# V weights loaded uncast by SyncE and cast on VectorE, in a linear-attention block on eight cores

## The reference

```python
q = phi(xn @ W_Q.T); k = phi(xn @ W_K.T); v = xn @ W_V.T      # 8 heads of 64; phi(u) = elu(u) + 1
S = gamma * S + k (outer) v;  z = gamma * z + k               # scan over the tokens, gamma = sigmoid(decay_log)
y = (S.T q) / (z . q + 1e-6) * sigmoid(xn @ W_g.T + b_g)
attn = y @ W_O.T
w = top-2 of softmax(xn @ gate_w.T)
ffn = xn @ W_lin.T + b_lin + sum over the two experts of w * (xn @ left_e) @ right_e     # rank 4
out = x + attn + ffn
```

## Time and profile before

| what | value |
|---|---|
| median of three runs | 260.21 us |
| the profiled execution's own time | 260.27 us |
| span of its slowest core (core 3) | 259.2 us |
| spans of the eight cores | 256.0 to 259.2 us |
| TensorE busy | 236.6 us (91%) |
| VectorE, ScalarE, GpSimd busy | 162.0, 75.5, 61.7 us |
| granted TensorE clock, all cores | 1.000 |

### The profile page before, as it was taken

How to read it: one execution, slowest core, us unless ns; L and a number is a source line. 1 busy time by engine, 2 the same in 40 slices (tenths; PEclk the granted TensorE clock), 3 DMA queues, 4 the chain that set the end, 5 groups by cost and what they waited for, 6 DMA issues and landing times.

```text
span 259.2 us, 5279 instructions; the slowest of 8 cores (256.0 to 259.2 us)
## 1 busy us (share of the span) xinstructions
PE 236.6 (91%) x1688; PEld 116.9 (45%) x1688; DVE 162.0 (63%) x425; ACT 75.5 (29%) x128; POOL 61.7 (24%) x99
## 2 busy tenths in 40 slices
PE   0238999999989999999999999999999999999995
PEld 0124354454545555454444455444545454445442
DVE  3743667658848678666555657556656776677522
ACT  2653766476163432314132021112110201000000
POOL 0790300012144421405050403021304030333000
PEclk9999999999999999999999999999999999999999
DMA  5999999999998046342435122223231315243423
GB/s 147 237 153 263 250 167 188 252 174 177 232 199 266 3 116 192 61 164 61 164 41 170 37 82 83 101 82 104 82 124 63 121 63 181 82 153 104 154 106 137
DMA packets 20366, 35.86 MB, mean 138 GB/s; under 512 B 12210, under 2 KB 12530, under 8 KB 20084
## 3 DMA queue, kind: packets, MB, share of 16 engines
q1 hardware_dynamic: 17444, 24.89, 32.0%
q0 software_dynamic: 2896, 10.64, 21.7%
HBM read 32.00 MB, written 8.39 MB: 156 GB/s over the span
## 4 chain that ended last, share of the span: by engine, by line
PE 85%; DMA 6%; DVE 3%; issue 2%; ACT 2%; DVEq 0%; ACTq 0%; POOLq 0%
PE PJ L367 27%; PE L L389 17%; PE L L433 9%; PE PJ L360 8%; DMA wv_sb<-wv 5%; PE PJ L389 4%; PE L L367 3%; PE PJ L433 2%; PE SY L381 2%; DMA x_sb<-x 2%; PE SY L405 2%; PE T L419 1%; PE SY L409 1%; PE T L338 1%; PE T L427 1%
## 5 line engine op out<-in xcount | busy, mean ns | idle before, releaser
L389 PE MATMUL L<-wlin_sb,xnfm 128*128 128x512 bf16 x208 | 49.2, 379 | 0.0
L325 POOL TENSOR_SCALAR S_blk<-S_sb,small_s 128x260 bf16<-128x260 f32 x30 | 28.6, 969 | 82.7 <-DVE S_sb L827 82.5
L389 PEld LDWEIGHTS L<-wlin_sb,xnfm 128*128 128x128 bf16 x208 | 20.0, 98 | 24.4 <-issue 1.0
L656 DVE TENSOR_SCALAR e_sb<-e_sb 128x512 bf16<-128x512 bf16 x32 | 9.7, 302 | 30.7 <-ACT e_sb L898 30.7
L898 ACT ACTIVATE e_sb<-PJ 128x512 bf16<-128x512 f32 x28 | 16.5, 593 | 40.5 <-PE PJ L367 39.4
L367 PE MATMUL PJ<-xnfm,wk_sb 128*128 128x512 bf16 x112 | 26.6, 380 | 1.2 <-ACT th_g L905 1.2
L874 ACT ACTIVATE xn_tm<-x_sb,nmr,rstd 128x1024 bf16<-128x1024 f32 x16 | 19.9, 1242 | 25.4 <-POOL nmr L281 23.9
L433 PE MATMUL L<-wo_sb,ygfm 128*128 128x512 bf16 x104 | 26.7, 379 | 0.0
L367 PE MATMUL PJ<-xnfm,wg_sb 128*128 128x512 bf16 x112 | 26.6, 379 | 0.0
L367 PE MATMUL PJ<-xnfm,wq_sb 128*128 128x512 bf16 x112 | 26.6, 380 | 0.0
L360 PE MATMUL PJ<-wv_sb,xnfm 128*128 128x512 bf16 x96 | 23.7, 389 | 2.5 <-DMA wv_sb<-wv 2.5
(11 more groups left out here) (122 smaller groups left out, 336.7 us busy)
## 6 DMA issues: line engine op xcount, KB each, us to landing
ro_sb<-x SPq DMA_DIRECT2D x16, 512.0 KB, 3.4
out<-ro_sb SPq DMA_DIRECT2D x15, 512.0 KB, 2.7
x_sb<-x SPq DMA_DIRECT2D x10, 512.0 KB, 8.4
x_sb<-x POOLq DMA_DIRECT2D x6, 512.0 KB, 21.6
wlin_sb<-wlin POOLq DMA_DIRECT2D x1, 2048.0 KB, 38.5
wv_sb<-wv POOLq DMA_DIRECT2D x4, 256.0 KB, 12.7
wq_sb<-wq POOLq DMA_DIRECT2D x2, 512.0 KB, 18.5
wk_sb<-wk POOLq DMA_DIRECT2D x2, 512.0 KB, 25.4
```

Of the source, the lines that this page charges most:

```text
L325: GP.tensor_scalar(S_blk[:, :].rearrange("p (q w) -> p q w", q=4)[:, :, 65 * e : 65 * e + 65], S_sb[:, :].rearrange("p (q w) -> p q w", q= ...
L389: TE.matmul(lb(c, n)[:, :], xnk(k, c), wlin_sb[:, D * k + 512 * n : D * k + 512 * n + 512], start=False, stop=False)
L656: VE.tensor_scalar(e_sb[:, 512 * i : 512 * i + 512], e_sb[:, 512 * i : 512 * i + 512], 1.0, None, ALU.min).then_inc(dv_m, 1)
```

## The change

The V weights no longer come through GpSimd's queue. SyncE loads them as fp32 in two halves of 1 MB each, one between x 2 and x 3 and one behind x 3, into the space of `wlin_sb`, which holds nothing yet. VectorE casts them in four quarters to `wv_sb` (`cast_wv`). The constants stand behind them on SyncE's queue. GpSimd's queue starts with the first half of Q once the first half of V has landed; W_lin and W_O wait for the four casts and are issued ahead of the two small copies. TensorE's V phase is ordered anew: chunks 0, 1 and 2 take the first half of the weights as they come, then all take the second. The work on constants is spread: the `nlg` steps stand around `xn(4)` and `xn(5)`, `dk8`, `gc4` and `dpq` behind the exponentials of Q, the eight exponent operations of the mask behind Q's last `phi` and ahead of `stats(6)`, and the mask's exponential behind `xn(7)` and ahead of K's first exponential. The first scores wait for the mask in the loop.

```diff
--- before.py
+++ after.py
@@ -88,6 +88,7 @@
     small = A("small_s", [128, 19], F32)
     cmat = th_g[:, 0:384]
     mtmp = th_g[:, 2048:3072]
+    wv32 = wlin_sb[:, :].bitcast(F32)
     bl32 = th_g[:, 3072:4096]
     nlg = A("nlg", [128, 12], F32)
     gc4 = A("gc4", [128, 4], F32)
@@ -136,13 +137,14 @@
     d_r = [sem(f"d_r{c}") for c in range(NCH)]
     d_id, d_sm, d_cm, d_bl = sem("d_id"), sem("d_sm"), sem("d_cm"), sem("d_bl")
     d_lg = sem("d_lg")
-    d_wv, d_wq, d_wk, d_wg = ([sem(f"d_wv{i}") for i in range(4)], [sem("d_wqa"), sem("d_wqb")],
+    d_wv, d_wq, d_wk, d_wg = ([sem("d_wva"), sem("d_wvb")], [sem("d_wqa"), sem("d_wqb")],
                               [sem("d_wka"), sem("d_wkb")], [sem("d_wga"), sem("d_wgb")])
     d_wl, d_wo, d_rt = sem("d_wl"), sem("d_wo"), sem("d_rt")
     pe_xtr, pe_v, pe_q, pe_k, pe_g = (sem("pe_xtr"), sem("pe_v"), sem("pe_q"), sem("pe_k"),
                                       sem("pe_g"))
     pe_tg, pe_tht, pe_ktr, pe_sc = sem("pe_tg"), sem("pe_tht"), sem("pe_ktr"), sem("pe_sc")
     pe_av, pe_st, pe_ytr, pe_o = sem("pe_av"), sem("pe_st"), sem("pe_ytr"), sem("pe_o")
+    dv_cast = sem("dv_cast")
     dv_ini, dv_st, dv_bn, dv_xev = sem("dv_ini"), sem("dv_st"), sem("dv_bn"), sem("dv_xev")
     dv_dec, dv_mk, dv_tgc = sem("dv_dec"), sem("dv_mk"), sem("dv_tgc")
     dv_one, dv_nm, ac_ln, dv_rt = sem("dv_one"), sem("dv_nm"), sem("ac_ln"), sem("dv_rt")
@@ -217,11 +219,18 @@
         def load_res(c):
             SY.dma_start(ro(c), x_d[128 * c : 128 * c + 128, :]).then_inc(d_r[c], 16)
 
+        def load_wv(hf):
+            o = 4 * FH * hf
+            SY.dma_start(wv32[:, o : o + 4 * FH],
+                         wv_d[:, o : o + 4 * FH]).then_inc(d_wv[hf], 16)
+
         load_x(0)
         load_x(1)
         SY.dma_start(ident[:, :], ident_d[:, :]).then_inc(d_id, 16)
         load_x(2)
+        load_wv(0)
         load_x(3)
+        load_wv(1)
         SY.dma_start(small[:, :], small_d[:, :]).then_inc(d_sm, 16)
         SY.dma_start(cmat, cmat_d[:, :]).then_inc(d_cm, 16)
         SY.dma_start(bl32[32:33, 0:512], blin_d[:, 0:512]).then_inc(d_bl, 16)
@@ -283,10 +292,7 @@
 
     def pool_program():
         GP.memset(mhalf[:, :], -0.5).then_inc(po_ini, 1)
-        GP.wait_ge(d_x[0], 16)
-        for i in range(4):
-            o = 2 * FH * i
-            GP.dma_start(wv_sb[:, o : o + 2 * FH], wv_d[:, o : o + 2 * FH]).then_inc(d_wv[i], 16)
+        GP.wait_ge(d_wv[0], 16)
         wload_half(wq_sb, wq_d, 0, d_wq)
         xload(4)
         xload(5)
@@ -306,14 +312,15 @@
                          blin_d[:, 512 * n : 512 * n + 512]).then_inc(d_rt, 16)
         xload(8)
         xload(9)
+        GP.wait_ge(dv_cast, 4)
+        wload(wlin_sb, wlin_d, d_wl)
+        wload(wo_sb, wo_d, d_wo)
         GP.wait_ge(po_ini, 1)
         GP.wait_ge(ac_dec, 3)
         GP.tensor_copy(gC[:, :].rearrange("p (q w) -> p q w", q=4),
                        gc4[:, :].unsqueeze(2).to_broadcast([128, 4, 65]))
         GP.tensor_copy(dpk[:, :].rearrange("p (h w) -> p h w", h=8),
                        dk8[:, :].unsqueeze(2).to_broadcast([128, 8, 64])).then_inc(po_dk, 1)
-        wload(wlin_sb, wlin_d, d_wl)
-        wload(wo_sb, wo_d, d_wo)
         rs(8)
         rs(9)
         for c in range(NCH):
@@ -484,18 +491,22 @@
         xtr(0)
         xtr(1)
         TE.wait_ge(dv_xev, 1)
+        for i in range(2):
+            TE.wait_ge(dv_cast, i + 1)
+            vproj(0, ring4[0], 2 * i, 2 * i + 2)
         xtr(2)
         TE.wait_ge(dv_xev, 2)
-        TE.wait_ge(d_wv[0], 16)
-        for c in range(4):
-            if c == 3:
-                xtr(3)
-            TE.wait_ge(dv_xev, c + 1)
-            vproj(c, ring4[c], 0, 2)
-        for i in range(1, 4):
-            TE.wait_ge(d_wv[i], 16)
-            for c in range(4):
-                vproj(c, ring4[c], 2 * i, 2 * i + 2)
+        vproj(1, ring4[1], 0, 4)
+        TE.wait_ge(dv_xev, 3)
+        vproj(2, ring4[2], 0, 4)
+        for i in range(2, 4):
+            TE.wait_ge(dv_cast, i + 1)
+            vproj(0, ring4[0], 2 * i, 2 * i + 2)
+        xtr(3)
+        vproj(1, ring4[1], 4, 8)
+        vproj(2, ring4[2], 4, 8)
+        TE.wait_ge(dv_xev, 4)
+        vproj(3, ring4[3])
         TE.wait_ge(d_wq[0], 16)
         for m in range(4):
             TE.wait_ge(ac_v, m + 1)
@@ -650,6 +661,11 @@
         VE.tensor_copy(xdst(c), TT[c % 2][:, :].rearrange("p (k w) -> p k w", k=KCH)
                        ).then_inc(dv_xev, 1)
 
+    def cast_wv(i):
+        o = 2 * FH * i
+        VE.wait_ge(d_wv[i // 2], 16)
+        VE.tensor_copy(wv_sb[:, o : o + 2 * FH], wv32[:, o : o + 2 * FH]).then_inc(dv_cast, 1)
+
     def phi(n, bank, dst, s):
         i = n % 2
         VE.wait_ge(ac_e, n + 1)
@@ -732,17 +748,29 @@
         stats(1)
         stats(2)
         xev_v(0)
+        cast_wv(0)
+        cast_wv(1)
+        xev_v(1)
         stats(3)
-        xev_v(1)
         xev_v(2)
+        cast_wv(2)
+        cast_wv(3)
         xev_v(3)
+        stats(4)
         VE.wait_ge(d_sm, 16)
         VE.tensor_scalar(gb_h[:, :], small[:, 0:4], 0.5, None, ALU.mult).then_inc(dv_ini, 1)
+        stats(5)
         VE.wait_ge(ac_dec, 1)
         VE.tensor_scalar(nlg[:, :], nlg[:, :], 1e15, None, ALU.min).then_inc(dv_dec, 1)
+        xev_v(4)
+        for m in range(2):
+            phi(m, ring4[m], fm(qfm, 0)[:, 512 * m : 512 * m + 512], dv_q)
         VE.wait_ge(ac_dec, 2)
         VE.tensor_scalar(dk8a[:, :], nlg[:, 0:8], small[:, 16:17], None,
                          ALU.mult).then_inc(dv_dec, 1)
+        xev_v(5)
+        for m in range(2, 4):
+            phi(m, ring4[m], fm(qfm, 0)[:, 512 * m : 512 * m + 512], dv_q)
         VE.wait_ge(d_cm, 16)
         for h in range(H):
             o = (h % 2) * 512 + (h // 2) * 128
@@ -750,17 +778,9 @@
                                           nlg[:, h : h + 1], cmat[:, 128:256],
                                           ALU.mult, ALU.add)
         ins.then_inc(dv_mk, 1)
-        stats(4)
-        stats(5)
-        xev_v(4)
-        for m in range(2):
-            phi(m, ring4[m], fm(qfm, 0)[:, 512 * m : 512 * m + 512], dv_q)
-        xev_v(5)
-        for m in range(2, 4):
-            phi(m, ring4[m], fm(qfm, 0)[:, 512 * m : 512 * m + 512], dv_q)
         stats(6)
         stats(7)
-        VE.wait_ge(ac_mk, 1)
+        VE.wait_ge(ac_dec, 3)
         qt(0)
         for m in range(4):
             phi(4 + m, ring4[(m + 2) % 4], fm(kfm, 0)[:, 512 * m : 512 * m + 512], dv_k)
@@ -789,6 +809,8 @@
             if c > 0:
                 VE.wait_ge(pe_st, c)
             VE.tensor_tensor(ktm_sb[:, :], ktile, dpk[:, :], ALU.mult).then_inc(dv_ktm, 1)
+            if c == 0:
+                VE.wait_ge(ac_mk, 1)
             VE.wait_ge(pe_sc, c + 1)
             VE.tensor_tensor(A_sb[:, 0:512], SYb[0][:, :], masks[:, 0:512], ALU.mult)
             VE.tensor_tensor(A_sb[:, 512:1024], SYb[1][:, :], masks[:, 512:1024],
@@ -923,10 +945,17 @@
         SE.activation(dum[:, :], one_c[:, :], AF.Exp)
         for c in range(4):
             xn(c)
+        for c in range(4):
+            vev(c, ring4[c])
+        xn(4)
         SE.wait_ge(dv_ini, 4)
         SE.activation(nlg[:, :], small[:, 4:16], AF.Exp, scale=-1.0).then_inc(ac_dec, 1)
+        xn(5)
         SE.wait_ge(dv_dec, 1)
         SE.activation(nlg[:, :], nlg[:, :], AF.Ln, bias=one_c[:, :]).then_inc(ac_dec, 1)
+        for m in range(4):
+            SE.wait_ge(pe_q, m + 1)
+            eexp(m, ring4[m])
         SE.wait_ge(dv_dec, 2)
         SE.activation(dk8[:, :], dk8a[:, :], AF.Exp)
         SE.activation(gc4[:, :], nlg[:, 8:12], AF.Exp, scale=-128.0)
@@ -935,19 +964,12 @@
             ins = SE.activation(dpq[:, 128 * p : 128 * p + 128], cmat[:, 256:384], AF.Exp,
                                 scale=nlg[:, 8 + p : 9 + p])
         ins.then_inc(ac_dec, 1)
-        SE.wait_ge(dv_mk, 1)
-        SE.activation(masks[:, :], mtmp, AF.Exp).then_inc(ac_mk, 1)
-        for c in range(4):
-            vev(c, ring4[c])
-        xn(4)
-        xn(5)
-        for m in range(4):
-            SE.wait_ge(pe_q, m + 1)
-            eexp(m, ring4[m])
         vev(4, ring4[0])
         vev(5, ring4[1])
         xn(6)
         xn(7)
+        SE.wait_ge(dv_mk, 1)
+        SE.activation(masks[:, :], mtmp, AF.Exp).then_inc(ac_mk, 1)
         for m in range(4):
             SE.wait_ge(pe_k, m + 1)
             eexp(4 + m, ring4[(m + 2) % 4])
```

## The result

The changed kernel takes 263.59 us, the median of four runs (263.19 to 263.66), against 260.02 before in the same runs: 1.0144 times as long, 95% interval 1.0115 to 1.0174. It is slower by 3.6 us, and just outside the predicted range of 257.8 to 263.2.

What follows compares the result with a forecast made beforehand. Bound: two transfers, then a chain almost wholly on TensorE. Q starting 3.5 us earlier and constants adding 3.6 gave +0.1: span 259.3, plus 1.07 makes 260.4 us, no change; range 257.8 to 263.2.

Steps and rivals of the forecast that it cites:

- V's gain: V's weights by the new loading: V starts at 14.7 instead of 18.61 and Q at 25.2, 3.5 us earlier.
- T: The moment TensorE starts Q: 28.67 on core 3 before, predicted 25.2, with 230.5 us behind it before.
- the sum: Earlier start of Q, -3.5 us, plus constants put in behind it, +3.6: +0.1, span 259.3, time 260.4.
- the third rival: V's second half lands late because GpSimd's queue starts within 1 us and takes turns: T 27.9, time 263.1; chance 0.15.
- The price of the constants: Constants on the chain from Q's last phi to G: 3.6 us against 0.15 to spare, delaying G by that.
- the first rival: Constants behind T fall into slack of VectorE and ScalarE: 256.8, or 258.9 where 1.5 us hides; chance 0.2.
- x 4: Input chunk 4 on GpSimd's queue: claimed to come 2.9 us earlier with that queue, with some 2 us or more to spare.
- G - T: Time from TensorE's first Q matmul to its first G matmul: 19.6 us before, predicted 23.1 to 23.2.
- The clock: TensorE's clock falls after idling ahead of G, slowing G's first matmuls: +1.7 us, time 262.1; a rival, chance 0.15.
- its cases: 261.5 is the top of the forecast's own range, T at 26.3; 262.1 is the rival where TensorE's clock falls.
- its own range: The forecast's range for T from 24.2 to 26.3: time 259.2 to 261.5.

Runs made afterwards that it cites:

- e10: Changed kernel with the mask's exponents behind qt(0), its exponential behind K's, and V's weights back on GpSimd's queue in DMA-cast quarters; 259.34 us, 0.9984 times before.
- e9: Changed kernel with the mask's exponents behind qt(0), its exponential behind K's, and Q's weights started once x 0 landed, not V's first half; 265.29 us.
- e3: Kernel before with only the changed kernel's order of constants, including the earlier issue of W_lin and W_O; V's weights as before; 264.76 us, 1.0200 times before.
- e6: Kernel before with the constants' new order, but the mask's exponents behind qt(0) and its exponential behind K's; 260.36 us, 1.0026 times before.
- e8: Changed kernel with the mask's exponents behind qt(0), its exponential behind K's, and x 4 loaded ahead of Q's first half; 258.06 us, 0.9911 times before.
- e2: Changed kernel with 7 useless matmuls behind xtr(6) and 9 behind xtr(7), keeping TensorE busy ahead of G; 261.29 us.
- e4: Changed kernel with only the mask's exponential moved behind K's four exponentials, its exponents still ahead of stats(6); 261.25 us.

## Why the prediction was wrong

**V's gain was right.** Predicted: V at 14.7, Q at 25.2, halves landing at 13.9 and 19.2. Measured on core 7: 15.24, 25.55, and casts beginning at 14.40 and 19.41 as the halves landed. Two casts took 1.29 us, so 0.7 each was right. In part the size was luck. The 3.5 us were counted from core 3, the latest of the kernel before both in V and in Q. In the mean of the eight cores V starts 1.6 us sooner (16.4 to 14.8) and Q 2.6 (27.3 to 24.7), and by e10 about half of the gain in T is the order of the V phase, which the sum didn't price. GpSimd's packets came behind SyncE's, and the third rival didn't happen. e9 shows that the mechanism was real; its price of 263.1 can't be held against e9's 265.3, as q0's packets begin at 11.23 on core 3 of e9 and the rival had them at 14.9.

**The price of the constants was right.** 3.6 us predicted; 23.20 - 19.59 = 3.6 in e3, and 3.36 against the 19.84 of e6. There was nothing to hide it, and the first rival, to which 0.2 was given, is out.

**x 4 was wrong.** The step "everything on q0 comes 2.9 us earlier ... Chunks 4 to 7, K and G shift alike and had some 2 us or more to spare". On core 7 `stats(4)` starts at 25.40, having waited 2.33 us. The same core in the kernel before:

```profile
25.31 0.69 DVE L639 BATCH_NORM_STATS2 bn<-x_sb 128x6 f32<-128x512 f32 x1 [0.55 <-DMA x_sb<-x]
```

So x 4 came no sooner at all: it lands at 23.8 to 26.3 over the cores before and 24.0 to 26.1 after, 24.7 in the mean of both. The first half of Q's weights came 0.5 us sooner on core 7 (23.9 to 23.4). There was nothing to spare either: four cores already waited for x 4 in the kernel before, 0.3 to 1.1 us, and core 3 had 0.5. What did come sooner was its user: VectorE was free for `stats(4)` at 23.07 instead of 24.76 on core 7, and at 22.87 instead of 26.82 on core 3. In both kernels as many bytes are read ahead of x 4, and the DMA engines of core 7 are busy for 94 to 110% of every 2 us from 8 to 24; that fits, though no run tests it alone. The late x 4 made G - T 23.71 instead of 23.2 on core 7 and up to 25.1 elsewhere. e8 takes it away.

**The clock was the failed step.** The sum added 3.6 us to the 230.5 behind T and left the clock at nothing; it was put as a rival with 0.15, beside the forecast. It was a consequence of the forecast: the prediction had itself worked out 4.5 us with 1 us of work on TensorE, and both kernels with that stretch (the changed one, e3) lost the clock on six to eight cores in every execution. The price was +1.7. The difference to e2's time is 2.3 us. Core 7 leaves 213.2 us behind G, against 211.3 on the same core both before and in e2; six other cores and those of e3 leave 212.0 to 212.5 against core 3's 210.9, 1.1 to 1.6 more. The prediction's 234.1 us behind T held only where the clock did (234.6 on core 5; 235.7 to 237.1 on the others). Against it the text set only that no such gap stood in the trace of before, which speaks for neither side.

The sum with what was measured, on core 7: 25.55 + 23.71 + 213.24 = 262.5. The prediction had 25.2 + 23.2 + 210.9 = 259.3. Of the 3.2 us between, 0.35 is T, 0.5 x 4, and 2.3 lies behind G: 2.0 of it the clock by the same core's 211.3, the rest a difference between cores, which leave 210.8 to 211.3 in the kernel before. The right total of these steps lay above the 261.5 and 262.1 that the text gave to its cases, because the clock's price was never added to a late T and a late x 4. (The low end of its own range is 259.4 by its terms, 24.2 + 234.1 + 1.07, not 259.2.)

## What to carry to other kernels

When work is moved, look for the tightest hand-over behind its new place and charge it in full; here 0.15 us of slack met 3.6 us of constants, and the same constants cost nothing a few instructions further on. When a step of your own sum opens an idle stretch on TensorE, the slow clock behind it belongs into the same sum and isn't a rival. And when a transfer gets its user sooner, look at what now arrives last: after V's weights it was x 4, and after x 4 a 9.5 KB constant at the end of the queue.

## What the runs showed of the hardware

- Two idle stretches ahead of G with one chunk of transposes between them, behind the dense matmuls of K: with 1.42 to 1.50 and 1.08 us the clock fell to 0.50 on four cores, with 1.13 to 1.47 and 1.08 it held on the other four (e4). With 0.99 to 1.50 and 2.02 us it fell on fifteen of sixteen cores (the changed kernel and e3). With fillers in these stretches it held on all eight (e2).
- Uncast, q1 alone moves 1.19 MB in 4 us of the changed kernel (10 to 14 us, 101% of the time of the DMA engines). With casting transfers beside it (e9, 12 to 16 us) the queues move equal packets, 88 and 89, and the casting ones take 74% of the time against 28% for the same number of bytes written.
- The first packet of GpSimd's first transfer came 2.3 to 3.8 us behind its issue in the changed kernel (core 7: issued at 14.90, first packet at 17.66) and 3.6 to 5.3 in the kernel before (core 3: 6.49 and 10.66), both times beside a busy SyncE queue.
